# A step table for the scan units of a two-block image kernel, with the first half's finish at step 31

## The chip, the cores and the metric

The kernel runs on one core of a Trainium2 chip. The metric is device time in microseconds (us), lower is better. Five engines work side by side, each through its own instruction stream in order: PE (TensorE, matmuls), DVE (VectorE), ACT (ScalarE), POOL (GpSimd) and SP (SyncE, which here only issues DMAs). They meet only at semaphores: an instruction that waits holds up all that stands behind it on its engine.

## The reference

Input `x` is 16 images of 192 channels x 32 x 32 pixels, so 1024 positions each. Two blocks follow one another, each with a group norm before it and a residual around it:

```python
x = x + _L0_conv_ref(_gn(x), ...)   # projection, 3x3 depthwise conv + silu, chunked SSD scan (8 chunks of 128), layer norm, gate, projection
x = x + _L1_conv_ref(_gn(x), ...)   # projection, softplus, selective scan over 1024 positions, projection
```

The selective scan of the second block keeps 192 x 16 states:

```python
h = exp(d_t[..., None] * A) * h + (d_t * x_t)[..., None] * b_t[:, None, :]
y_t = einsum('bdn,bn->bd', h, c_t)
```

## The kernel before

**Two images at once.** `run(b, ...)` on each engine does a pass: the second block of image b beside the first block of image b + 1. There are 18 passes: b = -1 (first block of image 0 only), b = 0 to 14 with both, b = 15 (scan of the last image only) and b = 16 (its end). A pass is a loop `for s in range(SLOTS)` over 48 steps on every engine; the order within a step is the order of the code. No engine waits for a step as such, only for the semaphores of what it needs.

**The scan of image b** is cut into 48 units of 128 rows (32 channels x 4 states) by 512 positions, 24 for each half of the positions. Before the change a unit belongs to the step of its own number. A unit i passes through four engines: ACT makes its decay (L958, an Exp) in step i; DVE makes its input `wr` (L1236) in step i and scans it into `hst` (L1249) in step i + 1; POOL multiplies by C into `hc` (L768) in step i + 2; and PE adds two finished units to the output with four matmuls `bank<-hc,sel` (`sum_states`, called in every even step for the units i - 4 and i - 3). Rings tie them: a decay home is free when the unit before in it has been scanned, `hst` has three buffers, so the scan of unit i also waits for `hc` of unit i - 3 and, in the first half, for the `carry` copy of unit i - 3. That copy (L999, one column, the state that the second half starts from) is made by ACT for unit i - 2 at the end of step i, behind everything else of the step. Decays of the units below 8, 31 to 35 and from 38 on lie in PSUM banks, the others in three SBUF buffers (`dec`).

**The first block of image b + 1** sets what else a step does. Steps 0 to 2: group norm scale `xna`, `xnb` (L1063) and nine projections ("fills"). Steps 3, 5, 7 and 10 (`CONV_AT`): the four convs on PE, 24 or 48 calls of wcv matmuls each; conv u from the third on waits until conv u - 2 has left its banks. One step later (4, 6, 8, 11) ACT takes each out of PSUM with four Silus (`copy_conv`, L817 and L820), behind a table load, and loads the Exp/Ln table again (L823). Steps 3 to 8 also make dt: DVE softplus in step 5, PE's cumulative sum `csum` (`bank<-da,upper`) in step 6, `lndt` and its copies on DVE in step 6, Ln and two Exps on ACT in step 6, `ncs` on DVE in step 8. Steps 13 to 36: the eight SSD chunks, two steps each. Steps 37 to 40: statistics and group norm for the second block (means on PE in step 37, variances in 38, `xna` in 40). Steps 40 to 46: eight projections (`bank<-xna,wt1a` and `bank<-xnb,wt1b`). Steps 42 to 45 (`EARLY_AT`): statistics of the next input image.

**Finishing image b** (`finish`) adds the residual and the output projection: matmuls `x1a,ident`; `y1a,wo1a` and `y1b,wo1b`; `x1b,ident`; `y1a,wo1a` and `y1b,wo1b` again, in four steps from `END_AT`: 37 for the first half, 10 of the next pass for the second.

Names used below: stage A is steps 0 to 12, up to the first row transposes of the SSD (L1382); stage B is the SSD up to the last statistics (`mv`); stage C is the rest of the pass.

## Time and profile before

| what | value |
|---|---|
| median of 3 runs | 3541.34 us (3494.55 to 3560.41) |
| profiled execution, its own time | 3522.22 us |
| its span | 3520.5 us, mean granted TensorE clock 0.921 |
| PE busy | 3085.5 us, 88% |
| DVE busy | 2682.1 us, 76% |
| ACT busy | 1843.2 us, 52% |
| POOL busy | 1774.9 us, 50% |
| DMA queues | 27.4% of 16 engines' span |

The engine times are sums over the whole span, in which the passes repeat. No engine is full over all of it; which one sets the pace is read stage by stage. Matmuls overlap one another in the pipeline, so the PE figure is not a share of its peak.

### The profile page before, as it was taken

What the parts mean: (1) busy time and instruction counts of PE and PEld (TensorE: products, weight loads), DVE (VectorE), ACT (ScalarE), POOL (GpSimd) and SP (SyncE); (2) the same over time, 40 slices, a digit from 0 to 9 for tenths busy, and PEclk for the clock granted to TensorE, in tenths of its full rate; (3) what the DMA queues carried; (4) which work ended last, traced back from release to release, by engine and by line L of the source; (5) the groups of instructions that cost most, each with busy time, mean ns of one, the idle gap of its engine ahead of it and who ended that gap; (6) DMA issues with size and microseconds to landing.
All of it is one profiled execution on the core that took longest, in us unless ns stands there. A gap on an engine that the chain in (4) does not pass through costs nothing. (4 is left out here: it accounts for less than half of the span.)

```text
span 3520.5 us, 59688 instructions
## 1 busy us (share of the span) xinstructions
PE 3085.5 (88%) x19488; PEld 1739.0 (49%) x19488; DVE 2682.1 (76%) x3980; ACT 1843.2 (52%) x4315; POOL 1774.9 (50%) x1347
## 2 busy tenths in 40 slices
PE   4988889998898998889898898988889998898965
PEld 2655446364453735447364453735446364453710
DVE  1448878788787867868789787878868788787887
ACT  1536464653646546464564646546464563746542
POOL 2216545464554535545364554646545464555655
PEclk9999999998999989989899989989999998999976
DMA  3032141423214142141423314142141423215131
GB/s 63 11 108 75 46 129 50 116 70 97 85 46 144 40 136 65 58 116 39 134 70 96 85 46 127 58 129 76 59 117 46 121 70 108 73 45 147 37 103 66
DMA packets 103726, 290.86 MB, mean 83 GB/s; under 512 B 24941, under 2 KB 26588, under 8 KB 103388
## 3 DMA queue, kind: packets, MB, share of 16 engines
q1 hardware_dynamic: 103388, 286.71, 27.4%
q8 instruction: 169, 2.77, 0.3%
q14 instruction: 169, 1.38, 0.1%
HBM read 181.84 MB, written 39.85 MB: 63 GB/s over the span
## 5 line engine op out<-in xcount | busy, mean ns | idle before, releaser
L768 POOL TENSOR_TENSOR hc<-hst,bcrep 128x512 f32<-128x512 f32 x768 | 1204.4, 1568 | 1165.7 <-DVE hst L1249 1118.7
L854 ACT ACTIVATE ssd<-bank,ncs 128x128 f32<-128x128 f32 x1536 | 439.4, 385 | 230.1 <-PE bank L1298 229.3
L1298 PE MATMUL bank<-hc,sel 128*32 128x512 f32 x1536 | 447.7, 668 | 99.8 <-POOL hc L768 99.1
L1236 DVE TENSOR_TENSOR wr<-durep,bcrep 128x512 f32<-128x512 f32 x768 | 530.3, 691 | 3.1 <-DMA bcrep<-bc_rows 3.1
L1249 DVE TENSOR_TENSOR_SCAN hst<-dec,wr 128x512 f32<-128x512 f32 x256 | 389.7, 1522 | 93.6 <-ACT carry L999 60.3
L1298 PE MATMUL bank<-ssd 128*128 128x32 f32 (+1 forms) x3296 | 459.8, 293 | 0.0
L1298 PEld LDWEIGHTS bank<-ssd 128*128 128x128 f32 x3296 | 409.1, 197 | 17.6 <-issue 12.8
L958 ACT ACTIVATE bank<-durep,aneg 128x512 f32<-128x512 f32 x368 | 254.0, 690 | 300.4 <-DVE hst L1249 284.6
L1298 PE MATMUL bank<-ssd,wcv 64*32 64x512 f32 x5376 | 349.4, 599 | 0.0
L1298 PE MATMUL bank<-xna,wt0a 128*128 128x128 f32 (+3 forms) x1088 | 299.3, 377 | 36.4 <-DVE xnb L1064 35.4
L1249 DVE TENSOR_TENSOR_SCAN hst<-bank,carry,wr 128x512 f32<-128x512 f32 x240 | 306.1, 1275 | 11.9 <-ACT bank L958 2.5
L958 ACT ACTIVATE dec<-durep,aneg 128x512 f32<-128x512 f32 x400 | 292.7, 737 | 6.6 <-DVE hst L1249 4.1
L709 POOL TENSOR_TENSOR ssd<-ssd,wend 128x384 f32<-128x384 f32 x112 | 182.0, 1625 | 223.3 <-ACT ssd L901 223.3
L887 ACT ACTIVATE ssd<-bank,nbc,nwc 128x128 f32<-128x128 f32 x384 | 147.8, 454 | 274.8 <-PE bank L1442 274.8
L1298 PE MATMUL bank<-xnb,wt0b 128*128 128x128 f32 (+3 forms) x1088 | 287.2, 367 | 0.0
L1382 PE MATMUL bank<-ident,csum 128*128 128x128 f32 x1536 | 241.3, 281 | 21.4 <-ACT ssd L854 16.3
L1115 DVE TENSOR_TENSOR ssd<-ssd,bank 128x1536 f32<-128x1536 f32 x128 | 223.5, 1746 | 29.9 <-PE bank L1298 24.4
L1382 PEld LDWEIGHTS bank<-ident,csum 128*128 128x128 f32 x1536 | 187.1, 141 | 116.0 <-issue 50.4
L1298 PE MATMUL bank<-ssd,wo 128*128 128x128 f32 (+1 forms) x1536 | 215.7, 283 | 32.2 <-DVE x1b L1128 32.2
L1298 PEld LDWEIGHTS bank<-xna,wt0a 128*128 128x128 f32 (+1 forms) x1088 | 175.8, 195 | 135.3 <-issue 86.1
L1098 DVE TENSOR_TENSOR ssd<-ssd,bank 128x384 f32<-128x384 f32 x128 | 70.9, 554 | 208.1 <-PE bank L1298 208.1
L1298 PEld LDWEIGHTS bank<-ssd,wo 128*128 128x128 f32 (+1 forms) x1536 | 180.2, 167 | 64.6 <-DVE x1b L1128 37.6
(186 smaller groups left out, 4937.8 us busy)
## 6 DMA issues: line engine op xcount, KB each, us to landing
durep<-scratch SPq DMA_DIRECT2D x192, 512.0 KB, 3.9
bcrep<-bc_rows SPq DMA_DIRECT2D x128, 512.0 KB, 5.1
ssd<-stage SPq DMA_DIRECT2D x384, 140.4 KB, 2.9
ssd<-bcst SPq DMA_DIRECT2D x128, 74.4 KB, 2.7
xa<-in_x_dram SPq DMA_DIRECT2D x16, 512.0 KB, 4.2
scratch<-u SPq DMA_DIRECT2D x32, 256.0 KB, 2.5
scratch<-delta SPq DMA_DIRECT2D x32, 256.0 KB, 2.8
out_dram<-x1a SPq DMA_DIRECT2D x16, 512.0 KB, 4.6
```

The costliest lines, as they stand in the source:

```text
L709: nc.gpsimd.tensor_tensor(xw[:, c % 2, :].rearrange("p (h d) -> p h d", d=HD), xtok[:, c % 2, 0:DI].rearrange("p (h d) -> p h d", d=HD), b ...
L768: nc.gpsimd.tensor_tensor(hc[:, i % CRING, :], hst[:, i % HRING, :], bcrep[:, g, 1, :], ALU.mult).then_inc(hc_ready.sem, 1)
L854: ins = nc.scalar.activation(att[:, c % 2, h, :], bank[ROW_BANKS[r]][:, k * Q:(k + 1) * Q], ACT.Exp, bias=ncs[:, c, h:h + 1])
L887: ins = nc.scalar.activation(yzt[:, c % 2, m, :], bank[B_CBT][:, (m + 1) * Q:(m + 2) * Q], ACT.Identity, bias=nbc[:, m:m + 1], scale=nwc[: ...
L958: nc.scalar.activation(decay_of(i), durep[:, j % SLOTS_DU, 0, :], ACT.Exp, scale=aneg1[:, g * NB + k:g * NB + k + 1]).then_inc(decay_ready ...
L1098: nc.vector.tensor_tensor(y0[:, c % 2, :], yint[:, c % 2, :], bank[B_XY][:, 0:DI], ALU.add).then_inc(y0_ready.sem, 1)
L1115: nc.vector.tensor_tensor(a, a, bc(bank[B_CBT][:, 0:Q].unsqueeze(1), [P, NH, Q]), ALU.mult).then_inc(att_ready.sem, 1)
L1236: nc.vector.tensor_tensor(wr[:, i % WRING, :], durep[:, j % SLOTS_DU, 1, :], bcrep[:, g, 0, :], ALU.mult).then_inc(w_made.sem, 1)
L1249: nc.vector.tensor_tensor_scan(hst[:, i % HRING, :], decay_of(i), wr[:, i % WRING, :], carry[:, g:g + 1] if hf else 0.0, ALU.mult, ALU.add ...
L1298: return nc.tensor.matmul(out, lhsT, rhs, start=start, stop=stop, skip_group_check=True)
L1382: nc.tensor.matmul(ps[:, k * Q:(k + 1) * Q], bc(csum[:, 0, c, h:h + 1], [P, P]), ident[:, :], start=(k == 0), stop=False, is_transpose=Tru ...
```

## The change

A table says which units belong to a step. 28 steps from 12 on have one unit each; the first 12 have 17, and the last 8 have three. Steps 4, 6, 8 and 11 have 3, 2, 2 and 2 units. All loops over units go through `UNITS_AT`; the order of work for a given unit is kept, but of a step with several units an engine does the first stretch of its per-unit work for all of them. On ACT that means all decays of the step, then the first block's work of that step, then all carry copies. Besides that: the finish of the first half begins in step 31 and stands behind the first block's work of its step; the small Exp and Ln for dt come before `copy_conv` in step 4; PE's cumulative sum moves from step 6 (after a sum of units) to step 5; the statistics of the next image move one step earlier; decays of units 8 and 9 go to PSUM and those of 31 to 35 and 38 to 41 to `dec`; and copying `y1a` waits for the last finish.

```diff
-SLOTS = UNITS
+STEPS = 48
+UNITS_IN_STEP = [1, 1, 1, 1, 3, 1, 2, 1, 2, 1, 1, 2] + 28 * [1] + [0, 1, 0, 1, 0, 0, 1, 0]
+UNITS_AT = [range(sum(UNITS_IN_STEP[:s]), sum(UNITS_IN_STEP[:s + 1])) for s in range(STEPS)]
...
-EARLY_AT = 42
+EARLY_AT = 41
...
-END_AT = (37, 10)
+END_AT = (31, 10)
...
+FRONT_UNITS, LAST_UNITS = 10, 42
...
-    if i < 8 or i >= 38:
+    if i < FRONT_UNITS or i >= LAST_UNITS:
         return i % 2
-    return 6 + i % 2 if 31 <= i < 36 else None
+    return None
...
-                for u, at in enumerate(CONV_AT):
-                    if s == at + 1:
-                        copy_conv(n, u)
                 if s == 4:
...
                     nc.scalar.activation(dtl[:, :, :], dte[:, :, :], ACT.Ln, bias=1.0).then_inc(dtl_ready.sem, 1)
+                for u, at in enumerate(CONV_AT):
+                    if s == at + 1:
+                        copy_conv(n, u)
...
-            def copy_wide(n, hf):
+            def copy_wide(n, hf, prev):
+                if hf or prev:
+                    act.wait_ge(o1_ps.sem, o1_ps.at(n, 2 * hf))
...
-                        decay(b, s, end, first)
+                        for i in UNITS_AT[s]:
+                            decay(b, i, end, first)
...
-                        if 2 <= s < HU + 2:
-                            act.wait_ge(scanned.sem, scanned.at(b, s - 1))
+                        for i in UNITS_AT[s]:
+                            if 2 <= i < HU + 2:
+                                act.wait_ge(scanned.sem, scanned.at(b, i - 1))
...
-                if s == 6:
+                if s == 5:
                     pe.wait_ge(da_ready.sem, da_ready.at(n, 1))
...
-                        if s == END_AT[0]:
-                            pe.wait_ge(scanned.sem, scanned.at(b, 36))
-                        finish(b, s, 0, par)
                     if first:
                         first_block(b + 1, s, end if scan else None)
+                    if scan:
+                        finish(b, s, 0, par)
```

The order on PE between the second and the third conv of a pass with both blocks (steps 5 to 7). The wcv rows are convs, `hc,sel` are sums of two units, `da` is the cumulative sum for dt. Before:

```order
L1298 MATMUL bank<-ssd,wcv 32x512 x24
L1298 MATMUL bank<-hc,sel 32x512 [waits hc_ready]
L1298 MATMUL bank<-hc,sel 32x512
L1298 MATMUL bank<-da,upper 128x96 [waits fill_copied,da_ready]
L1298 MATMUL bank<-da,ones 128x96
L1298 MATMUL bank<-ident 128x1 [waits im_landed1,conv_done]
L1298 MATMUL bank<-ssd,wcv 32x512 x48
```

And of the change:

```order
L1310 MATMUL bank<-ssd,wcv 32x512 x24
L1310 MATMUL bank<-da,upper 128x96 [waits fill_copied,da_ready]
L1310 MATMUL bank<-da,ones 128x96
L1310 MATMUL bank<-hc,sel 32x512 [waits hc_ready]
L1310 MATMUL bank<-hc,sel 32x512
L1310 MATMUL bank<-hc,sel 32x512 [waits hc_ready]
L1310 MATMUL bank<-hc,sel 32x512
L1310 MATMUL bank<-ident 128x1 [waits im_landed1,conv_done]
L1310 MATMUL bank<-ssd,wcv 32x512 x48
```

The cumulative sum now comes first, and two sums instead of one stand ahead of the third conv: before it was that of units 2 and 3, now those of units 4 and 5 and of units 6 and 7.

The order on ACT in steps 5 and 6, around the Silus of the second conv. `bank<-durep,aneg` are decays into PSUM, `carry<-hst` the carry copies. Before:

```order
L958 ACTIVATE bank<-durep,aneg 128x512 [waits scanned]
L999 COPY carry<-hst 128x1 [waits scanned]
L958 ACTIVATE bank<-durep,aneg 128x512 [waits scanned]
L820 ACT_TABLE_LOAD
L820 ACTIVATE bs<-bank,cb 32x512 [waits conv_ps]
...
L823 ACT_TABLE_LOAD
L874 ACTIVATE dtl<-dtl 128x96 [waits csum_ready]
L875 ACTIVATE cexp<-csum 128x192
L876 ACTIVATE wend<-wend 128x96
L999 COPY carry<-hst 128x1 [waits scanned]
```

And of the change:

```order
L964 ACTIVATE bank<-durep,aneg 128x512 [waits scanned]
L1009 COPY carry<-hst 128x1 [waits scanned]
L964 ACTIVATE bank<-durep,aneg 128x512 [waits scanned]
L964 ACTIVATE bank<-durep,aneg 128x512 [waits scanned]
L828 ACT_TABLE_LOAD
L828 ACTIVATE bs<-bank,cb 32x512 [waits conv_ps]
...
L831 ACT_TABLE_LOAD
L882 ACTIVATE dtl<-dtl 128x96 [waits csum_ready]
L883 ACTIVATE cexp<-csum 128x192
L884 ACTIVATE wend<-wend 128x96
L1009 COPY carry<-hst 128x1 [waits scanned] x2
```

Ahead of the Silus there are now the decays of units 8 and 9 where there was that of unit 6, and behind them the carries of units 6 and 7 where there was that of unit 4. The decay of unit 9 goes to the bank that unit 7's decay has, so it waits for the scan of unit 7.

The order on PE at the end of the statistics for the second block, from step 37 on. `mv` and `gq` are the means and variances. Before:

```order
L1298 MATMUL bank<-x1a,ident 128x512 [waits scanned]
...
L1298 MATMUL bank<-hc,sel 32x512 [waits hc_ready]
L1298 MATMUL bank<-hc,sel 32x512
L1298 MATMUL bank<-y1a,wo1a 128x512 [waits y1_copied,x1_ps]
L1298 MATMUL bank<-y1b,wo1b 128x512
...
L1298 MATMUL bank<-gq,ga 128x1 [waits gdev_ready]
...
L1298 MATMUL bank<-y1a,wo1a 64x512 [waits y1_copied,x1_ps]
L1298 MATMUL bank<-y1b,wo1b 64x512
L1298 MATMUL bank<-xna,wt1a 128x512 [waits xn_ready]
```

And of the change:

```order
L1310 MATMUL bank<-mv,ga 128x1 [waits stats_ready]
...
L1310 MATMUL bank<-xcm,diag1b 64x512 [waits p1_copied,y1_copied]
...
L1310 MATMUL bank<-gq,ga 128x1 [waits gdev_ready]
...
L1310 MATMUL bank<-hc,sel 32x512 [waits hc_ready]
L1310 MATMUL bank<-hc,sel 32x512
L1310 MATMUL bank<-xna,wt1a 128x512 [waits xn_ready]
```

The six groups of the finish are gone from this place; they stand in steps 31 to 34, between the gates and output projections of the last two chunks.

## Rows read from the trace of the kernel before

**Rows 1.** One line of code, L1063: count, ns least/median/most, first and last start.

```profile
L1063 DVE TENSOR_SCALAR xna<-xa,gm,gr x16: 811/1051/1909, 56.7 to 3179.2; 128x1024 f32<-128x1024 f32 x16
```

**Rows 2.** Stretches: us, busy PE, PEld, DVE, ACT, POOL (x), PEclk, DMA share, GB/s.

```profile
1281.90:1342.30 60.40, 55.51 (x459) 20.80 (x459) 39.85 (x48) 41.96 (x74) 24.13 (x16) 0.94 0.46 123
1342.30:1456.60 114.30, 102.39 (x659) 76.28 (x658) 93.61 (x152) 58.01 (x170) 68.27 (x54) 0.94 0.17 54
1456.60:1494.10 37.50, 33.73 (x100) 11.54 (x100) 32.90 (x50) 14.44 (x24) 17.88 (x13) 0.86 0.32 105
...
812.90:858.50 45.60, 41.77 (x100) 14.90 (x100) 32.77 (x49) 14.51 (x25) 16.90 (x12) 0.70 0.30 97
```

**Rows 3.** Timeline of PE, stage A: start us, us, operation [idle before <-releaser].

```profile
1310.88 5.36 PE L1298 MATMUL bank<-ssd,wcv 64*32 64x512 f32 x48
1316.16 1.05 PE L1298 MATMUL bank<-hc,sel 128*32 128x512 f32 x4
...
1317.91 5.38 PE L1298 MATMUL bank<-ssd,wcv 64*32 64x512 f32 x96
...
1326.98 1.05 PE L1298 MATMUL bank<-hc,sel 128*32 128x512 f32 x4 [2.71 <-POOL hc L768]
...
1329.71 6.43 PE L1298 MATMUL bank<-ssd,wcv 64*32 64x512 f32 x96
...
1342.29 0.65 PE L1382 MATMUL bank<-ident,csum 128*128 128x128 f32 x4
```

**Rows 4.** Timeline of DVE, stage A.

```profile
1316.87 1.28 DVE L1148 TENSOR_SCALAR dtl<-dt 128x96 f32<-128x96 f32 x1
...
1318.86 1.22 DVE L1249 TENSOR_TENSOR_SCAN hst<-bank,wr 128x512 f32<-128x512 f32 x1
...
1322.81 1.08 DVE L1155 TENSOR_TENSOR ncs<-dtl,csum 128x96 f32<-128x96 f32 x1 [0.17 <-ACT dtl L874]
...
1330.96 1.23 DVE L1249 TENSOR_TENSOR_SCAN hst<-dec,wr 128x512 f32<-128x512 f32 x1 [2.37 <-ACT carry L999]
```

**Rows 5.** Timeline of ACT, stage A.

```profile
1316.41 0.69 ACT L958 ACTIVATE bank<-durep,aneg 128x512 f32<-128x512 f32 x1 [1.91 <-DVE hst L1249]
1317.12 1.28 ACT L820 ACT_TABLE_LOAD   x1
1318.41 0.68 ACT L820 ACTIVATE bs<-bank,cb 32x512 f32<-32x512 f32 x1
...
1322.94 0.27 ACT L876 ACTIVATE wend<-wend 128x96 f32<-128x96 f32 x1
1323.11 0.18 ACT L999 COPY carry<-hst 128x1 f32<-128x1 f32 x1
```

**Rows 6.** Timeline of POOL, stage A.

```profile
1320.16 1.64 POOL L768 TENSOR_TENSOR hc<-hst,bcrep 128x512 f32<-128x512 f32 x1 [2.08 <-DVE hst L1249]
```

**Rows 7.** Timeline of PE and of DVE, end of stage B.

```profile
1451.23 1.73 PE L1298 MATMUL bank<-ssd,wo 128*128 128x128 f32 x12 [1.70 <-DVE x1b L1128]
...
1454.82 0.28 DVE L1127 TENSOR_TENSOR x1a<-bank,xa 128x128 f32<-128x128 f32 x1
```

**Rows 8.** Timeline of PE, stage C.

```profile
1459.61 2.08 PE L1298 MATMUL bank<-y1a,wo1a 128*128 128x512 f32 x2
...
1462.67 0.38 PE L1298 MATMUL bank<-gq,ga 128*128 128x1 f32 x2
...
1469.23 1.12 PE L1298 MATMUL bank<-xna,wt1a 128*128 128x512 f32 x2
...
1487.74 0.38 PE L1298 MATMUL bank<-gq,ga 128*128 128x1 f32 x2 [2.21 <-DVE gq L1055]
```

**Rows 9.** Timeline of DVE, stage C.

```profile
1456.64 0.20 DVE L1047 BATCH_NORM_AGGREGATE mv<-st 128x2 f32<-128x12 f32 x1
...
1460.14 0.16 DVE L1055 TENSOR_TENSOR gq<-gd,mv 128x2 f32<-128x2 f32 x1
...
1465.80 1.76 DVE L1063 TENSOR_SCALAR xna<-x1a,gm,gr 128x1024 f32<-128x1024 f32 x1
```

More of the change, by code:

```diff
@@ L771, in run @@
             def run(b, par, scan, end, first, more):
-                for s in range(SLOTS if scan or first else 2):
-                    if s < 2:
-                        if end:
-                            states_by_c(b - 1, UNITS - 2 + s, False)
-                    elif scan:
-                        states_by_c(b, s - 2, end)
+                for s in range(STEPS if scan or first else 2):
+                    for i in UNITS_AT[s]:
+                        if i < 2:
+                            if end:
+                                states_by_c(b - 1, UNITS - 2 + i, False)
+                        elif scan:
+                            states_by_c(b, i - 2, end)
                     if scan:
@@ L987, in run @@
                 mid_step = Steps(act, act_mid_steps, b)
-                for s in range(SLOTS if scan or first else END_AT[1] + END_STEPS):
+                for s in range(STEPS if scan or first else END_AT[1] + END_STEPS):
                     if scan:
-                        decay(b, s, end, first)
+                        for i in UNITS_AT[s]:
+                            decay(b, i, end, first)
                     if scan:
@@ L1577, in finish, with sums @@
                     mm(o, wo1b[r, c], y1b[r, :], False, True).then_inc(o1_ps.sem, 1)
-            def run(b, par, scan, end, first, more):
-                for s in range(SLOTS if scan or first else END_AT[1] + END_STEPS):
-                    if s in (0, BATCH):
-                        if end:
-                            sum_states(b - 1, BATCHES - 2 + s // BATCH, False)
-                    elif scan and s > 2 and (s - 2) % BATCH == 0:
-                        sum_states(b, (s - 2) // BATCH - 1, end)
-                    for hf in range(2):
-                        if scan and s == hf * HU + WIDE + 3:
-                            start_rest(b, hf)
+            def sums(b, i, scan, end):
+                if i in (0, BATCH):
+                    if end:
+                        sum_states(b - 1, BATCHES - 2 + i // BATCH, False)
+                elif scan and i > 2 and (i - 2) % BATCH == 0:
+                    sum_states(b, (i - 2) // BATCH - 1, end)
+                for hf in range(2):
+                    if scan and i == hf * HU + WIDE + 3:
+                        start_rest(b, hf)
+            def run(b, par, scan, end, first, more):
+                for s in range(STEPS if scan or first else END_AT[1] + END_STEPS):
+                    for i in UNITS_AT[s]:
+                        sums(b, i, scan, end)
                     if end:
                         if scan and s == END_AT[1]:
-                            pe.wait_ge(scanned.sem, scanned.at(b, 8))
+                            pe.wait_ge(scanned.sem, scanned.at(b, FRONT_UNITS))
                         if not scan and s == END_AT[1]:
```

40 lines of the change are left out of this document (21 added, 19 removed).

## Prediction, made before the changed kernel ran

> **What bounds the kernel now.** The busy shares come first. No engine is full, so the next view is the passes: sixteen starts of `xna` from `xa`, one for each pass from b = -1 to 14 [rows 1]. From the first start, 56.7, to the last, 3179.2, it is 208 us a pass, the short first one (no scan) among them. I cut one pass with both blocks (b = 5, 212.2 us) into its stages [rows 2]. Stage A takes 60.4 us and PE is busy for 55.5 of them; there PE sets the pace. Stage B, the SSD, takes 114.3 us, PE 102.4 and DVE 93.6: the two hand chunks to each other. Stage C takes 37.5 us, and DVE is busy for 32.9, PE for 33.7. The granted clock matters in C: in the pass from 644.6 on the same stage took 45.6 us at 0.70 against 37.5 at 0.86 [rows 2]. Whatever is gained or lost below happens in 15 passes (b = 0 to 14).
>
> The timeline of stage A shows how it is driven. PE does a conv in 5.4 us and then a sum of two units in 1.05, back to back, with one hole: 2.71 us before the sum at 1326.98, where `hc` was late [rows 3]. `hc` is late because DVE and ACT hold one another up. ACT's Silus of a conv take a table load of 1.28, four times 0.68 and a second load; only behind them come the small Exps and the carry copy [rows 5], and DVE stands idle for such a carry, 2.37 us at 1330.96 [rows 4]. So a scan three units ahead of a carry can't run during the Silus. That is what the added units run into.
>
> **Stage A, step by step, in times of this pass.** Up to the end of the first conv (1308.6) nothing changes. Then PE has one more sum than before ahead of the second conv, so this ends at 1317.2 and not at 1316.24 [rows 3], and the cumulative sum, which took about 0.65 between 1317.2 and the next conv's start [rows 3], ends at 1317.85.
>
> DVE: the scan of unit 5 needs the carry of unit 2, behind the first Silus, which is there at about 1313.1. The scan (1.22), `wr` (0.67), five small operations of dt (an estimate of 1.4), the scan of unit 6 and its `wr` take DVE to 1318.3. Then `lndt`, which took 1.28 and ended with POOL's `hc`; here POOL starts the `hc` of unit 6 at about 1317.7 and holds it until 1319.3. From the end of `lndt` to the next scan it took 0.71, in which the cumulative sum is copied and subtracted [rows 4]. So unit 7 is scanned from 1320.1 to 1321.3, and its `hc` (1.64, [rows 6]) ends at 1323.0. PE has done the sum of units 4 and 5 by 1318.9 and must wait for that `hc` in order to do the sum of 6 and 7 ahead of the third conv: **4.1 us idle**. After the sum the third conv starts at 1324.3, not at 1317.91 [rows 3].
>
> ACT: the decay of unit 9 waits for the scan of unit 7 (1321.3) and takes 0.7; then come load, Silus, load (1.28 + 2.8 + 1.28), the three small ones (0.75) and the carry of unit 6 (0.18) [rows 5]. That makes 1328.5. DVE scans unit 9 then (to 1329.8) and POOL's `hc` ends at 1331.5. PE is through with the third conv at 1329.7, or about 1330.8 if it runs as slowly after its hole as the fourth did after the hole of 2.71 (6.43 against 5.38, [rows 3]); I take 1330.8, so **0.7 idle** before the sum of 8 and 9, which ends at 1332.6. On DVE `ncs` waits for POOL (1.08 where its neighbours take 0.25, [rows 4]), until 1331.8; then two scans with a `wr` between them, 1.9 to 2.8 each, put the `hc` of unit 11 at 1337.5: **4.9 idle** before the sum of 10 and 11. The fourth conv follows the first matmul of the finish, and ends at 1346.8 where it was 1336.14 [rows 3]. One sum more than before (two in place of one) follows until the first row transposes. They start at 1354.1, not at 1342.29 [rows 3]. Stage A loses **11.8 us**: three more sums, 3.15, and 7.0 more idle (9.7 less the old 2.71), 1.1 for the slow conv, and half a microsecond of rounding. From below: without the wait of `lndt` for POOL, without a slow conv and with the quickest scans it is 8. From above, with ACT and DVE half a microsecond later in each link, 14.
>
> One price is disputed, that of a table load. Here the Silu starts 0.01 after its load of 1.28 ends [rows 5]. By the Trainium skill, "ScalarE: Activation LUTs", What ACT_TABLE_LOAD costs, a switch of sets is the load and a drain of 1.38 us as well, some 2.66 together. By that rule the two switches on the chain would add 2.8 us a pass and 41 us in all; no gap of that size stands behind this load, so the sum goes by the row.
>
> **Stage B.** The number of units in a step stays as it was. The first half's finish, 6.4 us of PE at full clock, now stands in steps 31 to 34. PE had holes there, 1.70 before the last output projection for instance [rows 7]. Laid among them, the six groups make that projection end 3.5 later; the residual that waited for it started 1.86 after its old end of 1452.96 [rows 7], so 1.7 remains. I take **+1.8**, between 0 (the holes hold it all) and 3.
>
> **Stage C.** The finish no longer stands before the variances: `gq` was ready at 1460.30 [rows 9] and PE came to it at 1462.67, behind `y1a,wo1a` [rows 8]. 2.3 of that go at once. Then the `xna` of 1465.80 [rows 9] and the projections that could start only at 1469.23, behind another two groups of the finish [rows 8], come sooner: I get 3.7 us from the last statistics to the first projection, and more in passes where the clock is low there, as in the C of 45.6 us [rows 2]. From the first projection to the end it was 24.9 [rows 2, 8], with eight projections of 2.05, four sums, a start of the second accumulation and the two statistics of the next image. The new order has two sums less inside it and no such start, and DVE has 5 units (1.95 each) less to do, which makes 22 to 22.5: PE still waits for `gq` of the next image, about 2.7 where it was 2.21 [rows 8], since softplus, `u1` and one scan come first on DVE. Stage C gains 3.7 and 2.5, **6.2 us**. From below 3.5, if only the finish's way is saved; from above 9.6, if all PE waits go.
>
> **Sum.** 11.8 + 1.8 - 6.2 = +7.4 us a pass, by 15 passes 111 us. 3522 + 111 = 3633 us. That stands against the profiled execution's 3522.22; the median of the runs is 19 us above it, which would make 3652. I say 3635.
>
> **Rivals.**
>
> *PE never waits in A.* If ACT and DVE ran so far ahead that the sums of step 7, 8 and 10 found their `hc`, A would lose only the three sums and win the old 2.71. With B and C as above that is 3.15 - 2.71 + 1.8 - 6.2 = -4.0 a pass, 3463 us; with C at its best of 9.6 it is -7.4, 3412 us, over 3% faster. It decides at one point: the decay of unit 9 would have to be made without the cumulative sum's copy on DVE ahead of it. Against it: that copy stands before the scan of unit 7 in DVE's order, and the decay is queued before the Silus on ACT. 0.05.
>
> *Half of it.* The holes come out shorter, A loses 4 to 8, C gains 6 to 9: between -5 and +3 a pass, so 3450 to 3570, no change that can be told. For it: DVE is busy for only 39.9 of A's 60.4 us [rows 2], so some of what I lay on it may fit in earlier. 0.20.
>
> *The clock falls.* The new holes, 4.1 and 4.9, are longer than the 2.71 after which a conv took 6.43. If the third and fourth conv ran at 1.2 and not 2.4 GHz throughout, each would take 10.8: 4.3 and 5.4 more than my sum has, 9.7 a pass, 3780 us. The Trainium skill, "TensorE: Matmul & The Clock Gate", What's actually happening, has the array fall to half rate after idling, as that row does. For it the rows of stage C at 0.70; against it the sums and the conv between the holes. 0.09.
>
> *My sum.* 0.66.
>
> **The numbers.** About 2% is what a measurement of this kernel can tell. Range: from 3545, which leaves out the first rival and most of the second, to 3725, where A is at 14, C at 3.5 and B at 3 (+13.5 a pass). That keeps about eight cases in ten. Slower by over 2% is my sum but for its lowest part, and the clock: 0.72. Within 2%: 0.23. Faster: 0.05.
>
> **What would show it.** In stage A: PE idle for 3 to 5 us before the sum ahead of the third conv and again before the one ahead of the fourth, with POOL's `hc` as releaser; the Silus of the second conv about 5 us later after their conv than now; first row transposes at 70 to 74 us from the pass's start instead of 60.4. In stage B nothing but a longer end. In stage C `gq,ga` within 0.2 us of `gq`, and 30 to 33 us in all. I would be wrong if the sums of units 6, 7 and 10, 11 start without a wait, or if the stretch from the first row transposes to the last statistics shrinks, which nothing in these rows provides for.

## The result: 3.5% slower, and the profile after

| what | before | after |
|---|---|---|
| median | 3535.4 us (4 runs, 3494.6 to 3560.4) | 3655.7 us (4 runs, 3651.3 to 3661.7) |
| ratio | | 1.0352, 95% interval 1.0310 to 1.0394 |
| span of the profiled execution, granted clock | 3520.5, 0.921 | 3649.5, 0.895 |
| PE busy | 3085.5 | 3107.1, 85% |
| DVE busy | 2682.1 | 2750.8, 75% |
| ACT, POOL busy | 1843.2, 1774.9 | 1847.8, 1753.3 |

The change costs 129 us in the profiled execution. No engine got much more to do; what grew is the time in which they wait for one another. In the tables of this document a stage is the mean over the 14 passes b = 0 to 13, from the start of `xna` to the next start, taken from the starts in the traces. C1 is the stretch from the last statistics to the first projection, C2 the rest of C. "Low" is how many us of a pass PE was granted half the clock, worked out from the granted clock of four stretches in each pass (length x (1 - clock) x 2). "Masking" is DVE's multiplication `ssd<-ssd,bank` of 128x1536, one for each chunk of the SSD.

| kernel | A | B | C1 | C2 | pass | low |
|---|---|---|---|---|---|---|
| before | 60.1 | 109.6 | 14.5 | 26.3 | 210.4 | 28 |
| after | 73.5 | 114.1 | 10.2 | 20.8 | 218.6 | 40 |

So A lost 13.5, B lost 4.6, C gained 9.8: 8.2 a pass, 115 in 14 passes. The first pass, b = -1, got shorter (177.1 to 166.5), and what follows the sixteenth `xna` got 25.5 longer (341.2 to 366.8). Together 129.

The pass b = 10 of after, in four stretches: A; the start of B up to the masking of the third chunk; the rest of B; C. Columns: stretch, its us, PE busy (instructions), granted clock, DMA share, GB/s. It answers to [rows 2].

```profile
2405.70:2480.00 74.30, 62.75 (x471) 0.86 0.54 142
2480.00:2513.20 33.20, 27.24 (x144) 0.85 0.25 87
2513.20:2593.20 80.00, 77.22 (x526) 1.00 0.10 28
2593.20:2624.20 31.00, 26.50 (x78) 0.78 0.23 72
```

PE's timeline in stage A of this pass, which answers to [rows 3]. Columns: start, us, operation, idle before it and its releaser.

```profile
2435.83 5.36 PE L1310 MATMUL bank<-ssd,wcv 64*32 64x512 f32 x48
2442.36 0.46 PE L1310 MATMUL bank<-da,upper 128*128 128x96 f32 x2 [1.17 <-DVE da L1155]
...
2442.97 1.05 PE L1310 MATMUL bank<-hc,sel 128*32 128x512 f32 x4
2448.93 1.92 PE L1310 MATMUL bank<-hc,sel 128*32 128x512 f32 x4 [4.91 <-POOL hc L775]
...
2451.30 6.92 PE L1310 MATMUL bank<-ssd,wcv 64*32 64x512 f32 x96
2458.16 1.05 PE L1310 MATMUL bank<-hc,sel 128*32 128x512 f32 x4
2463.04 1.92 PE L1310 MATMUL bank<-hc,sel 128*32 128x512 f32 x4 [3.83 <-POOL hc L775]
2464.89 2.08 PE L1310 MATMUL bank<-x1a,ident 128*128 128x512 f32 x2
...
2467.11 5.85 PE L1310 MATMUL bank<-ssd,wcv 64*32 64x512 f32 x96
```

The two foretold holes are there: 4.91 ahead of the third conv and 3.83 ahead of the fourth, both for POOL's `hc`. The matmuls behind each run slowly: sums of 1.92 where they take 1.05, a conv of 6.92 where it takes 5.38. What makes `hc` late stands on ACT and DVE, [rows 4, 5] of before. First ACT, around the Silus of the second conv:

```profile
2439.95 0.17 ACT L1009 COPY carry<-hst 128x1 f32<-128x1 f32 x1
2443.51 0.69 ACT L964 ACTIVATE bank<-durep,aneg 128x512 f32<-128x512 f32 x1 [3.39 <-DVE hst L1259]
2447.21 0.69 ACT L964 ACTIVATE bank<-durep,aneg 128x512 f32<-128x512 f32 x1 [3.01 <-DVE hst L1259]
2447.92 1.28 ACT L828 ACT_TABLE_LOAD   x1
2449.22 0.68 ACT L828 ACTIVATE bs<-bank,cb 32x512 f32<-32x512 f32 x1
...
2453.92 0.27 ACT L1009 COPY carry<-hst 128x1 f32<-128x1 f32 x2
```

And DVE in the same stretch:

```profile
2438.06 1.22 DVE L1259 TENSOR_TENSOR_SCAN hst<-bank,wr 128x512 f32<-128x512 f32 x1 [6.72 <-ACT carry L1009]
...
2439.78 1.27 DVE L1079 TENSOR_SCALAR dtu<-dte 128x96 f32<-128x96 f32 x1
...
2443.97 1.27 DVE L1158 TENSOR_SCALAR dtl<-dt 128x96 f32<-128x96 f32 x1
...
2454.12 1.22 DVE L1259 TENSOR_TENSOR_SCAN hst<-bank,wr 128x512 f32<-128x512 f32 x1 [4.47 <-ACT carry L1009]
...
2459.17 2.11 DVE L1259 TENSOR_TENSOR_SCAN hst<-dec,wr 128x512 f32<-128x512 f32 x1
...
2477.41 1.23 DVE L1259 TENSOR_TENSOR_SCAN hst<-dec,wr 128x512 f32<-128x512 f32 x1 [4.37 <-ACT carry L1009]
```

ACT waits 3.39 and 3.01 for scans before it may make the next decays, and its Silus are queued behind those decays: they end at 2452.0, although their conv ended at 2441.2. DVE in turn waits 6.72, 4.47 and 4.37 for carry copies that stand behind the Silus. On the mean of 14 passes such waits make 15.3 us of stage A on DVE, where they made 4.3 before. In the page of the whole execution the scans with a decay in PSUM and no carry input have 208.4 us of idle before them, 167.6 of it for a carry:

```profile
L1259 DVE TENSOR_TENSOR_SCAN hst<-bank,wr 128x512 f32<-128x512 f32 x160 | 195.5, 1222 | 208.4 <-ACT carry L1009 167.6
L1310 PE MATMUL bank<-hc,sel 128*32 128x512 f32 x1536 | 458.3, 700 | 195.9 <-POOL hc L775 195.9
```

PE's timeline at the border of B and C, for [rows 8]:

```profile
2593.50 0.38 PE L1310 MATMUL bank<-mv,ga 128*128 128x1 f32 x2 [2.02 <-DVE mv L1058]
...
2594.48 1.97 PE L1310 MATMUL bank<-xcm,diag1b 128*64 128x512 f32 x2
2596.89 0.59 PE L1310 MATMUL bank<-gq,ga 128*128 128x1 f32 x2 [0.44 <-DVE gq L1065]
...
2603.36 2.08 PE L1310 MATMUL bank<-xna,wt1a 128*128 128x512 f32 x2 [2.76 <-DVE xnb L1074]
```

No finish stands in the way any more: the variances run as soon as `gq` is there.

### The profile page after: what moved, and what is told of

Read it like the earlier page. It is cut to its first block and busy times, and to the rows that moved or that the text cites. A ratio compares the mean times of both kernels' runs of the same rounds, so it can differ in the third digit from the quotient of the medians.

```text
span 3649.5 us, 59703 instructions
## 1 busy us (share of the span) xinstructions
PE 3107.1 (85%) x19488; PEld 1756.8 (48%) x19488; DVE 2750.8 (75%) x3980; ACT 1847.8 (51%) x4315; POOL 1753.3 (48%) x1347
## 3 DMA queue, kind: packets, MB, share of 16 engines
q14 instruction: 169, 1.38, 0.1%
## 5 line engine op out<-in xcount | busy, mean ns | idle before, releaser
L1310 PE MATMUL bank<-ssd 128*128 128x32 f32 (+1 forms) x3296 | 481.1, 301 | 2.1 <-DVE ssd L1125 1.9
L1310 PEld LDWEIGHTS bank<-ssd 128*128 128x128 f32 x3296 | 433.5, 207 | 11.4 <-issue 5.5
L1259 DVE TENSOR_TENSOR_SCAN hst<-dec,carry,wr 128x512 f32<-128x512 f32 x288 | 408.0, 1417 | 20.6 <-ACT dec L964 10.0
L964 ACT ACTIVATE dec<-durep,aneg 128x512 f32<-128x512 f32 x512 | 368.3, 731 | 69.0 <-DMA durep<-scratch 49.8
L1310 PE MATMUL bank<-ssd,wcv 64*32 64x512 f32 x5376 | 368.1, 630 | 0.0
L1259 DVE TENSOR_TENSOR_SCAN hst<-bank,wr 128x512 f32<-128x512 f32 x160 | 195.5, 1222 | 208.4 <-ACT carry L1009 167.6
L964 ACT ACTIVATE bank<-durep,aneg 128x512 f32<-128x512 f32 x256 | 175.9, 691 | 278.9 <-DVE hst L1259 249.7
L716 POOL TENSOR_TENSOR ssd<-ssd,wend 128x384 f32<-128x384 f32 x112 | 141.8, 1266 | 285.4 <-ACT ssd L909 285.4
L1394 PE MATMUL bank<-ident,csum 128*128 128x128 f32 x1536 | 256.0, 293 | 13.7 <-ACT ssd L862 10.7
L1310 PEld LDWEIGHTS bank<-xna,wt0a 128*128 128x128 f32 (+1 forms) x1088 | 173.6, 194 | 173.1 <-issue 110.5
L1310 PEld LDWEIGHTS bank<-hc,sel 128*32 128x32 f32 x1536 | 56.6, 114 | 391.6 <-POOL hc L775 275.2
```

What stands on the lines that cost most here:

```text
L716: nc.gpsimd.tensor_tensor(xw[:, c % 2, :].rearrange("p (h d) -> p h d", d=HD), xtok[:, c % 2, 0:DI].rearrange("p (h d) -> p h d", d=HD), b ...
L964: nc.scalar.activation(decay_of(i), durep[:, j % SLOTS_DU, 0, :], ACT.Exp, scale=aneg1[:, g * NB + k:g * NB + k + 1]).then_inc(decay_ready ...
L1259: nc.vector.tensor_tensor_scan(hst[:, i % HRING, :], decay_of(i), wr[:, i % WRING, :], carry[:, g:g + 1] if hf else 0.0, ALU.mult, ALU.add ...
L1310: return nc.tensor.matmul(out, lhsT, rhs, start=start, stop=stop, skip_group_check=True)
L1394: nc.tensor.matmul(ps[:, k * Q:(k + 1) * Q], bc(csum[:, 0, c, h:h + 1], [P, P]), ident[:, :], start=(k == 0), stop=False, is_transpose=Tru ...
```

## The experiments

Each was timed beside the kernel before on the same chip; the ratio is to that. All stage values follow in one table.

| run | median us | ratio (95%) | A | B | C1 | C2 | pass | low | last part |
|---|---|---|---|---|---|---|---|---|---|
| before | 3535.4 | 1 | 60.1 | 109.6 | 14.5 | 26.3 | 210.4 | 28 | 341.2 |
| after | 3655.7 | 1.035 (1.031 to 1.039) | 73.5 | 114.1 | 10.2 | 20.8 | 218.6 | 40 | 366.8 |
| e1, old table | 3460.5 | 0.976 (0.971 to 0.981) | 58.2 | 112.6 | 10.2 | 25.3 | 206.3 | 27 | 354.6 |
| e2, carry first | 3499.2 | 0.988 (0.983 to 0.993) | 67.5 | 110.3 | 10.2 | 20.6 | 208.6 | 28 | 356.0 |
| e3, copies behind | 3647.2 | 1.030 (1.026 to 1.035) | 72.6 | 114.7 | 10.2 | 21.0 | 218.5 | 41 | 370.8 |
| e4, Silu first | 3560.4 | 1.006 (1.000 to 1.012) | 72.4 | 111.1 | 10.2 | 20.6 | 214.2 | 35 | 365.3 |
| e5, e1 + carry first | 3485.9 | 0.987 (0.980 to 0.994) | 58.8 | 114.0 | 10.3 | 25.3 | 208.4 | 32 | 351.4 |
| e6, three moves | 3552.4 | 1.007 (1.003 to 1.010) | 69.7 | 110.5 | 10.2 | 20.9 | 211.3 | 36 | 361.8 |
| e7, e1, finish at 37 | 3593.0 | 1.017 (1.011 to 1.024) | 61.0 | 115.9 | 12.3 | 26.3 | 215.5 | 42 | 355.3 |
| e8, three units | 3492.2 | 0.990 (0.984 to 0.996) | 64.3 | 109.9 | 10.8 | 22.7 | 207.8 | 34 | 353.4 |
| e9, e7, decays in PSUM | 3532.9 | 0.998 (0.996 to 1.001) | 60.7 | 112.9 | 11.8 | 26.5 | 211.8 | 34 | 344.9 |
| e10, busy holes in A | 3635.7 | 1.029 (1.023 to 1.035) | 72.3 | 114.2 | 10.2 | 20.8 | 217.5 | 30 | 360.1 |
| e11, e1, busy in C | 3471.6 | 0.980 (0.974 to 0.986) | 58.5 | 114.4 | 12.1 | 22.9 | 207.9 | 22 | 351.4 |
| e12, e2 + Silu first | 3503.7 | 0.989 (0.985 to 0.993) | 67.0 | 110.4 | 10.2 | 20.6 | 208.1 | 28 | 352.1 |

### The table alone

```diff
-UNITS_IN_STEP = [1, 1, 1, 1, 3, 1, 2, 1, 2, 1, 1, 2] + 28 * [1] + [0, 1, 0, 1, 0, 0, 1, 0]
+UNITS_IN_STEP = 48 * [1]
-FRONT_UNITS, LAST_UNITS = 10, 42
+FRONT_UNITS, LAST_UNITS = 8, 38
```

> The change with one unit in every step (48 times 1) and decays in PSUM for units below 8 and from 38 on; the finish stays in steps 31 to 34, the statistics of the next image a step early. Theory (the loss of stage A is the units laid on steps 4, 6, 8 and 11): stage A is back at 60 us a pass from 73.5; from the last statistics to the first projection 10 to 11 us stay from 14.5, since that gain is the finish's; the rest of stage C goes back towards 26 (24 to 26), since that gain is the units'. B 110 to 112. Sum 206 to 209 a pass, 3440 to 3500 us in all. Rival (the tail's gain is the finish's alone): the rest of C stays at 21 and the whole comes to under 3420. Rival (the moved finish costs as much in B as it saves): 3520.

With the table go back the homes of the decays of units 8, 9 and 38 to 41. Measured: 3460.5. The rest of the change is a gain of 2.4%, the lowest median of all versions; the table takes 195 us away from it. A falls from 73.5 to 58.2, C2 rises by 4.6 only: the table pays 15.4 us in A, and 1.5 in B, for 4.6 in C.

### Three moves inside the new table

The carry copies come out from behind the Silus:

```diff
                         for i in UNITS_AT[s]:
                             decay(b, i, end, first)
+                            if 2 <= i < HU + 2:
+                                act.wait_ge(scanned.sem, scanned.at(b, i - 1))
+                                nc.scalar.copy(carry[:, i - 2:i - 1], hst[:, (i - 2) % HRING, HALF - 1:HALF]).then_inc(carried.sem, 1)
```

> The change, but ACT makes each carry copy right behind the decay of its unit's slot, ahead of the first block's work of the step (so ahead of the Silus). Theory: the scans of units 5, 9 and 16 no longer wait for a carry behind the Silus (6.7, 4.5 and 4.4 us idle on DVE); PE's hole before the sum ahead of the third conv shrinks from 4.9 to 2.6, since that one hangs on the cumulative sum; the one ahead of the fourth stays at about 4, since units 10 and 11 stand behind ncs. Stage A 67 to 69 from 73.5, 3565 us (3540 to 3590). Rival (the carries are not what holds DVE, its decays are): no change, 3650.

Measured 3499.2. DVE's waits for a carry in stage A fall from 15.3 to 2.7 us a pass, PE's hole ahead of the third conv from 4.9 to 2.8 on the mean (2.6 expected). A is 67.5, inside what was expected, and the time is 66 us below the expectation because B gave back its loss too (114.1 to 110.3) and the last part 10.8. One move of a copy of 0.2 us takes 156 us off the changed kernel.

On DVE the cumulative sum's copies of step 6 move behind the scans:

```diff
-                if s == 6:
-                    step(nc.vector.tensor_scalar(lndt[:, :, :], dt0[:, :, :], TINY, None, ALU.max))
...
+                    if first and s == 6:
+                        cumulative(b + 1, step)
```

> The change, but on DVE in step 6 lndt, the copy of the cumulative sum and wend stand behind the scans of units 7 and 8. Theory: unit 7 is scanned 2 us earlier, PE's hole ahead of the third conv is 2.9 instead of 4.9, all behind it comes 2 us earlier: stage A 71.5, 3620 us. Rival (that hole is the Silus' doing, not the cumulative sum's): hole and time unchanged, 3650.

Measured 3647.2: a miss, nothing to speak of. The hole ahead of the third conv did shrink as expected, to 3.2, and that conv starts 8.2 after the second's end where it was 10.1, but the fourth starts 9.1 after the third's end where it was 8.8, and B is as long as in the changed kernel. My point of decision for the rival in which PE never waits, the copy ahead of the scan of unit 7, wasn't what decides.

On ACT the Silus of the second conv move ahead of the decays of step 6:

```diff
+                    if first and s == CONV_AT[1] + 1:
+                        copy_conv(b + 1, 1)
                     if scan:
                         for i in UNITS_AT[s]:
                             decay(b, i, end, first)
```

> The change, but on ACT in step 6 the Silus of the second conv stand ahead of the decays of units 8 and 9. Theory: the hole ahead of the third conv stays (4.9), the Silus come 6 us sooner after their conv, unit 9 is scanned 4 us sooner, and the hole of 3.8 ahead of the fourth conv goes. Stage A 69 to 70, 3590 us. Rival (both holes are one delay by DVE): both stay, 3650.

Measured 3560.4, better than expected, but not where it was expected. PE's timeline in stage A of this kernel:

```profile
2421.14 1.92 PE L1312 MATMUL bank<-hc,sel 128*32 128x512 f32 x4 [4.92 <-POOL hc L775]
...
2429.84 2.17 PE L1312 MATMUL bank<-hc,sel 128*32 128x512 f32 x8
...
2433.12 5.38 PE L1312 MATMUL bank<-ssd,wcv 64*32 64x512 f32 x96
2440.15 1.05 PE L1312 MATMUL bank<-hc,sel 128*32 128x512 f32 x4 [1.65 <-POOL hc L775]
...
2445.72 1.57 PE L1312 MATMUL bank<-hc,sel 128*32 128x512 f32 x4 [1.41 <-POOL hc L775]
```

The first hole stays at 4.92, the second is gone, and new ones of 1.65 and 1.41 open behind the fourth conv, 3.3 us a pass on the mean: A keeps 72.4. The gain lies in B, 3.0 us, of which 2.7 in its start, where the granted clock is 0.891 in place of 0.845. So the two holes have two causes, the first the carries and the second the late Silus, and removing one moves the wait.

All three together:

```diff
+                            if 2 <= i < HU + 2:
...
+                        copy_conv(b + 1, 1)
...
+                        cumulative(b + 1, step)
```

> The table of the change with the three moves together: carries behind the decays, Silus of the second conv ahead of the decays of step 6, the cumulative sum's copies behind the scans of step 6. Each alone gave 3499.2, 3560.4 and 3647.2 against 3655.7 of the changed kernel. Theory (two holes with two causes: carries for the first, late Silus for the second): they add up for the most part, A from 73.5 to 63 to 66, B near 110, C at 30.7, a pass of some 205, 3450 to 3480. Rival (one chain through DVE and ACT, which each move only shortens at one end): nothing is gained over the best one, 3500, A stays at 67.5.

Measured 3552.4, outside both ranges. The first hole is gone, but ACT's timeline shows what the three together do:

```profile
2381.37 0.18 ACT L1005 COPY carry<-hst 128x1 f32<-128x1 f32 x1
2384.48 0.28 ACT L882 ACTIVATE dtl<-dtl 128x96 f32<-128x96 f32 x1 [2.93 <-DVE wend L1148]
...
2385.10 0.71 ACT L964 ACTIVATE dec<-durep,aneg 128x512 f32<-128x512 f32 x1
```

The Ln for dt waits 2.93 for `wend`, which DVE now makes behind its scans, and the decays of step 7 and 8 are queued behind it; the fourth conv starts 14.2 after the third's end. One run more tells whether it is that:

```diff
+                            if 2 <= i < HU + 2:
...
+                        copy_conv(b + 1, 1)
```

> The changed kernel with two of the three moves: carries behind the decays, and the Silus of the second conv ahead of the decays of step 6; the cumulative sum's copies stay ahead of the scans. With all three moves the time was 3552.4, worse than the 3499.2 of the carries alone: the third conv then began 2.0 us after the second's end, without a hole, but the fourth 14.2 after the third's end (7.1 with carries alone). Theory (the copies put behind the scans make the Ln and Exps of dt late on ACT, and with them everything queued behind them, the carries too): without that move the fourth conv starts 5 to 8 us after the third's end, A at 65 to 68, 3470 to 3500. Rival (the Silus ahead of the decays do the harm as soon as the carries are early): the gap of 14 stays, A near 70, 3540 to 3560.

Measured 3503.7, A 67.0, the fourth conv 6.5 after the third: the copies behind the scans did the harm, and the Silus ahead of the decays add nothing once the carries are early.

### The old table again, and a milder one

```diff
-UNITS_IN_STEP = [1, 1, 1, 1, 3, 1, 2, 1, 2, 1, 1, 2] + 28 * [1] + [0, 1, 0, 1, 0, 0, 1, 0]
+UNITS_IN_STEP = 48 * [1]
...
+                            if 2 <= i < HU + 2:
```

> The table of one unit a step again, the finish at step 31, and on ACT each carry copy right behind the decays of its step. In the run with the old table alone (3460.5) the fourth conv still started 4.4 us after the third had ended, where a sum takes 1.05. Theory (the carry copies behind the Silus hold DVE's scans back, whatever the table): stage A falls from 58.2 to 55.5 to 57, B by 1 to 2, so about 3 us less in each of 15 passes: 3415 to 3435. Rival (only a step with several units makes a carry late; with one unit a step the wait lies under PE's work): A stays within 0.5 us, and the time at 3460.

Measured 3485.9, ratio 0.987 against 0.976 of the old table alone: the rival held for A (58.8 against 58.2), and the time is no better. With one unit a step a late carry lies under PE's work. The 25 us on top are not in a wait of that kind: B's start took 32.0 in place of 30.5, at a clock of 0.864 in place of 0.929.

```diff
+UNITS_IN_STEP = [1, 1, 1, 1, 2, 1, 1, 1, 1, 1, 1, 2, 2] + 27 * [1] + [0, 1, 1, 1, 0, 0, 1, 1]
+FRONT_UNITS, LAST_UNITS = 8, 42
```

> A milder table, three units moved in place of five, into steps 4, 11 and 12 ([1,1,1,1,2,1,1,1,1,1,1,2,2], 27 ones, [0,1,1,1,0,0,1,1]), so that no second unit stands in the Silu steps 6 and 8; carries behind the decays as in the run beside it with the old table. Theory (a unit taken out of C is worth 0.9 us there and costs half a sum, 0.5, in A, as long as it doesn't stand in steps 6 and 8): A 1.5 to 3 us longer than with the old table and carries first, C 2 to 3 shorter, the time within 20 us of it. Rival (any unit moved into the front makes the holes again): A longer by 5 or more, 3460 or above, 30 us or more over the old table with carries first.

Measured 3492.2, within 20 us of the old table with early carries, as the theory said, but by larger terms than it had: A is 5.5 longer (64.3), which is the rival's term, B 4.1 shorter and C 2.0 shorter. PE waits before the fourth conv are gone (it starts 2.0 after the third's end), and 4.3 us of waiting for `hc` stand behind it. So the units are no cheaper outside steps 6 and 8; the wait only comes later.

### What the finish does, and what the decays do

```diff
-END_AT = (31, 10)
+END_AT = (37, 10)
```

(with the old table)

> The table of one unit a step and the finish of the first half back at step 37, so that of the change only the small moves are left (cumulative sum in step 5, dt ahead of the Silus, statistics one step earlier, decays of units 31 to 35 in SBUF, finish behind the first block's work). Theory (the finish's place is what shortens the way from the last statistics to the first projection, 14.5 to 10.2, and costs B something): that stretch returns to 13.5 to 14.5, B falls from 112.6 to 110 to 111, the pass from 206.3 to 207.5 to 209, the time 3480 to 3505. Rival (the gain is the small moves'): 3460, as with the finish at step 31.

Measured 3593.0, far above both. C grows by 3.1, as C1 goes from 10.2 to 12.3 and C2 by 1.0. C1 keeps the other half of its gain over the 14.5 of before, with the finish behind the block's work: the means and variances go ahead of it, and its last two matmul pairs now run behind the first projections. But B gets longer too, 115.9, and A, 61.0, with the same work. Both go with the clock: PE is at half clock for 42 us a pass here and for 27 with the finish at 31. On the mean the first conv starts 25.1 after the pass's start, at a granted clock of 0.78 up to there, and not 22.3, at 0.88; the start of B takes 33.7 in place of 30.5.

The end of B was not helped. From the last chunk's masking to the last statistics it took 22.7 in before, 25.4 after, and 25.3 here, with the finish away. Hence the next one, which adds to this one only:

```diff
-    return None
+    return 6 + i % 2 if 31 <= i < 36 else None
...
+                if first and i == 31:
+                    act.wait_ge(row_exp.sem, row_exp.at(n + 1, NRB * NCH))
...
+                        if s == END_AT[0]:
+                            pe.wait_ge(scanned.sem, scanned.at(b, 36))
```

> As the run with the old table and the finish back at step 37 (3593.0), but the decays of units 31 to 35 lie in PSUM again, as before the change. In every variant so far, with the finish at 31 or at 37, it took 25.1 to 25.5 us from the start of the last chunk's masking on DVE to the last statistics, where before it took 22.7; so the finish, on which my sum laid 1.8 us of stage B, can't be it. Theory (the scans of units 31 to 35 with both inputs in SBUF are slower beside POOL, and hold DVE up where it sets the pace): that stretch returns to 22.5 to 23.3 and the time falls by 2 to 3 us a pass, to 3545 to 3565. Rival (it is something else that all variants share, such as the finish behind the first block's work): the stretch stays at 25 and the time at 3593.

The two added waits belong to the place: the banks are used by the first block's work and by the finish. Measured 3532.9, 60 us less and below the expected range, and the stretch is back at 22.7. DVE's scans in it, one pass with the decays in SBUF (columns: group, count, busy us, mean ns, idle before):

```profile
L1259 DVE TENSOR_TENSOR_SCAN hst<-dec,carry,wr 128x512 f32<-128x512 f32 x7 | 11.6, 1651 | 0.2
```

and one with them in PSUM:

```profile
L1261 DVE TENSOR_TENSOR_SCAN hst<-bank,carry,wr 128x512 f32<-128x512 f32 x5 | 6.3, 1270 | 0.1
L1261 DVE TENSOR_TENSOR_SCAN hst<-dec,carry,wr 128x512 f32<-128x512 f32 x2 | 2.6, 1280 | 0.1
```

11.6 us of scans against 8.9: the 2.7 us by which B's end was longer. A pass is 3.7 shorter; the 1.0 beyond that lies in C1, A and the start of B. The last part of the execution, in which only scans are left, falls from 355.3 to 344.9 with it.

### Is it the clock?

Matmuls that compute nothing fill the holes of the changed kernel:

```diff
+                        if first and scan and i == 10:
+                            pe.wait_ge(conv_done.sem, conv_done.at(b + 1, 2))
+                            keep_busy(CONV_BANKS[2][0], 4)
+                        if first and scan and i == 14:
+                            pe.wait_ge(conv_done.sem, conv_done.at(b + 1, 4))
+                            keep_busy(CONV_BANKS[3][0], 3)
                         sums(b, i, scan, end)
```

> The changed kernel, its order untouched, with matmuls that compute nothing laid into PE's two holes: four of about 0.87 us ahead of the sum of units 6 and 7 (hole of 4.9) and three ahead of the sum of 10 and 11 (hole of 3.8). In the changed kernel the granted clock of stage A is 0.894 (before 0.940), that from the first row transposes to the third chunk's masking 0.845 (before 0.946), and that stretch takes 33.5 us where it takes 28.8 in passes of before at 1.00. Theory (PE's idle time in the holes is what brings the clock down, in A and behind it): third and fourth conv 5.4 in place of 6.6 and 5.8, the stretch behind at 28 to 30, a pass 4 to 7 us shorter, 3550 to 3595. Rival (the clock at the start of B falls for the idle time there, before the state matmuls): stage A shortens by 1 us, the stretch stays at 33, 3640. A third way (more work brings it down further): 3655 or above.

PE's timeline, the fillers being `wcv,ident`:

```profile
2438.32 1.05 PE L1310 MATMUL bank<-hc,sel 128*32 128x512 f32 x4
2439.30 3.70 PE L1310 MATMUL bank<-wcv,ident 128*128 128x512 f32 x8
2444.28 1.05 PE L1310 MATMUL bank<-hc,sel 128*32 128x512 f32 x4 [1.28 <-POOL hc L775]
2445.26 0.38 PE L1310 MATMUL bank<-ident 128*128 128x1 f32 x2
2445.57 5.38 PE L1310 MATMUL bank<-ssd,wcv 64*32 64x512 f32 x96
2452.45 1.05 PE L1310 MATMUL bank<-hc,sel 128*32 128x512 f32 x4 [1.49 <-POOL hc L775]
2453.43 2.84 PE L1310 MATMUL bank<-wcv,ident 128*128 128x512 f32 x6
2458.37 1.29 PE L1310 MATMUL bank<-hc,sel 128*32 128x512 f32 x4 [2.09 <-POOL hc L775]
```

Measured 3635.7: the rival's value. The third conv runs at 5.38 now and A's clock is 0.956 in place of 0.894, but A shortens by 1.2 only, since `hc` comes no sooner, and the start of B stays at 33.5 with a clock of 0.856. So the idle time in A's holes does bring the clock down in A, that is worth about 1 us a pass, and filling it does nothing for B. PE's wait for the first state matmul of B, the idle time that the rival names, was not filled and stays at 3.33 to 4.62.

The same in stage C of the fastest version:

```diff
                 if s == PRE_AT + 1:
+                    if again is not None:
+                        keep_busy(5, 3)
                     group_means(n, 1)
...
                         if k == 0:
+                            if again is not None:
+                                keep_busy(5, 2)
```

> The fastest variant so far (table of one unit a step, finish at 31; 3460.5) with matmuls that compute nothing in front of two waits of stage C: three ahead of the means of the last statistics (idle 3.1 us) and two ahead of the first projection (1.35). There C runs at a granted clock of 0.78 and its first projections take 2.05 where others take 1.1. Theory (idle time brings the clock down): C at 0.88 or above, its projections at 1.1 to 1.3, C 1.5 to 4 us shorter than 35.5, and a stage A behind it that begins at the full clock: 3400 to 3440. Rival (the clock there follows something else, or the added matmuls only stand in the way): C stays within 1 us of 35.5 and the time at 3450 to 3480.

Measured 3471.6. C's clock rose from 0.778 to 0.893 as expected; C shortened by 0.5 us only, the rival's line. C2 fell by 2.4 and C1 rose by 1.8: the fillers stood in the way of the variances and sums. And B's start was slow in 9 of 14 passes, 32.3 on the mean against 30.5. Matmuls that compute nothing do raise PE's clock, but this kernel gains little by it where DVE or ACT set the pace.

## Why the prediction was right, and where its terms were off

**The whole.** 3635 was forecast, 3655.7 measured, inside the range; slower, as the likeliest case. Against the profiled execution's own time of 3651.3 the sum gave 3633. The terms behind it are less good than the total: 11.8 + 1.8 - 6.2 forecast, 13.5 + 4.6 - 9.8 measured, +8.2 for +7.4. Misses of 1.7, 2.8 and 3.6 us a pass cancel, so that the total came this close is in good part luck; that A's loss outweighs C's gain is not.

**Stage A, 11.8 forecast, 13.5 measured.** The mechanism held: e1 takes it away with the table (15.4 us), e2 takes 6.1 away with the place of the carries alone. The added idle time was nearly right in sum: 10.5 us before the cumulative sum and the sums of units on the mean of 14 passes, 2.7 in before, so 7.8 more for the 7.0 forecast. Its parts were less so: 4.1, 0.7 and 4.9 forecast, 4.9, 0 and 4.2 on the mean (4.91 and 3.83 in the pass shown), and 1.2 before the cumulative sum that I didn't have. There `dtu` took 1.27 on DVE, beside POOL's `hc`, where I had laid all five dt operations at 1.4; they took 2.4. The rest of the difference is clock: two sums at 1.92 in place of 1.05, and a third conv of 6.6 in place of 5.4 on the mean; I had slowed one conv by 1.1 and no sum. The Silus of the second conv end 10.1 after it on the mean (10.8 in the pass shown), where they ended 4.2 after it: 5.9 later, about 5 forecast. The row transposes start 74.3 after the pass's start, 73.5 on the mean (70 to 74 forecast).

**Stage B, 1.8 forecast, 4.6 measured, by another cause.** This is the step that failed. I laid the finish's groups among PE's holes at the end of B; e7, with the finish back at step 37, has 25.3 us there, e1 with the finish at 31 has 25.5, and all variants with those decays in SBUF have 25.1 to 25.5. e9 shows what it is: the decays of units 31 to 35 in SBUF, 2.7 us. I named that move in the change and priced it at nothing. The other 1.9 is the start of B: up to the third chunk 33.5 for 30.2, at a clock of 0.845 for 0.946, of which the chunks between give 1.5 back. The late carries reach into it. DVE leaves stage A late (its wait of 4.37 at 2477.41 above), and PE waits for the first state matmul:

```profile
2490.95 0.91 PE L1310 MATMUL bank<-state,cs_ 128*128 128x384 f32 x2 [3.43 <-DVE state L1089]
```

That wait is 3.33 to 4.61 us in the 14 passes, 2.38 to 2.78 in before. In e2, with the carries early, it is 1.22 to 1.68 in 13 of 14 passes, and the start of B takes 30.1 at a clock of 0.922. In the changed kernel the clock falls in every pass, during this wait or within 1.5 us behind it. So my sum had no term for what A's delay does to B. Whether it is this wait that brings the clock down, no run shows by itself.

**Stage C, -6.2 forecast, -9.8 measured.** C1 gained 4.3 for the 3.7 forecast. In e7 and e9, where the finish stands at step 37 but behind the block's work, C1 is 2.2 and 2.7 shorter than in before and C2 no shorter; so about half of C1's gain goes with that order and the other small moves, and the rest with the finish's leaving C. The 5.5 of C2 had 2.5 in the sum: 4.6 are the table's (e1), where PE is busy for 19.8 us in place of 23.7. The term with the wrong sign is PE's wait for `gq` of the next image, which I raised from 2.21 to 2.7. It is 0.9 on the mean, and 2.2 in before: that alone is 1.8 of the 3.0 that I missed. I had put softplus, `u1` and a scan ahead of it on DVE. But it isn't the units taken out in front of it either, since with the old table (e1) the wait is 0.9 as well, here 1.01:

```profile
1440.14 0.38 PE L1310 MATMUL bank<-gq,ga 128*128 128x1 f32 x2 [1.01 <-DVE gq L1065]
```

What e1 and the changed kernel share and before lacks is, above all, the statistics one step earlier. That this is the cause is a reading; no run changed it alone.

**What the sum did not have.** The 15 passes were taken as equal. The first got 10.6 shorter, the last part 25.5 longer than before, though my term for it held only one pass of 7.4. About 10 of that are the decays in SBUF, by e7 and e9. 12 more go with the table (366.8 against 354.6). At the start of the last image's second pass DVE's timeline has this:

```profile
3496.89 1.28 DVE L1259 TENSOR_TENSOR_SCAN hst<-bank,carry,wr 128x512 f32<-128x512 f32 x1
3506.05 0.69 DVE L1246 TENSOR_TENSOR wr<-durep,bcrep 128x512 f32<-128x512 f32 x1 [7.88 <-DMA bcrep<-bc_rows]
```

I read it as part of those 12: e2 and e3, with the new table, have such a wait too (7.38 and 7.22), and e1, e7 and e9 have none. No run took it away alone.

**The rivals.** PE never waits: it waited, and e3 and e6 show that the copy which I made its turning point doesn't decide. Half of it: A lost more than 8. The clock falls: the two convs did not run at 1.2 GHz throughout, 6.6 and 5.8 against the 10.8 of that case. Yet the clock was a larger part than my 1.1 us: half clock for 40 us a pass, 28 before. The Trainium skill, "TensorE: Matmul & The Clock Gate", What's actually happening, has the array fall to half rate after idling; e10 agrees for the convs behind the holes (5.38 once filled), and [rows 3] did so before.

**The table load.** Behind the load of 1.28 at 2447.92 the first Silu starts at 2449.22, 0.02 after its end. A drain of 1.38 beside it, as the Trainium skill, "ScalarE: Activation LUTs", What ACT_TABLE_LOAD costs, has it, does not show here, neither behind the load nor ahead of it, where the decay ends 0.02 before it starts. Half of the 128 loads of this trace have the next instruction within 0.02 us of their end.

## What to carry to other kernels

When a schedule table moves more units of one chain into a step, look at what its engines queue behind other work in that step: a copy of 0.2 us behind Silus held DVE for 4 to 7 us, and moving the copy was worth 156 us. Read each buffer that changes its memory as a change of price, too: five decays that moved from PSUM to SBUF to make room for the better placed finish cost 60 us in the two runs that differ by them and the waits that go with their place. And test the parts of a bundle singly: the parts without the table were 2.4% faster than before, the whole was 3.5% slower.

## What the runs showed of the hardware

**A scan's time depends on where its decay lies.** With the decay in PSUM all 3904 scans of the 14 traces take 1.21 to 1.29 us, whether POOL is at work or not. With `dec` in SBUF it is 1.20 to 1.29 where POOL isn't at work when the scan starts (2596 scans), and up to 2.15, 1.67 on the mean, where it is (4252 scans). At 2459.17 above it is 2.11. POOL's `hc` ran from 2458.66 to 2460.20 there:

```profile
2458.66 1.54 POOL L775 TENSOR_TENSOR hc<-hst,bcrep 128x512 f32<-128x512 f32 x1 [1.58 <-DVE hst L1259]
```

The scan began 1.03 before that end and took 0.90 longer than the 1.21 of a scan beside an idle POOL. The Trainium skill, "SBUF — State Buffer", Who interferes with whom, says that a VectorE instruction with two SBUF inputs contends with a GpSimd instruction that reads SBUF, and that the later one is blocked until the other ends. These rows agree, for the scan too.

**The clock falls in one pass and not in another after the same idle time.** Two passes of before, PE at the start of B. In the first the state matmul comes after 2.48 us of idle, at full clock:

```profile
1134.96 1.05 PE L1298 MATMUL bank<-hc,sel 128*32 128x512 f32 x4
1138.48 0.91 PE L1298 MATMUL bank<-state,cs_ 128*128 128x384 f32 x2 [2.48 <-DVE state L1079]
```

and in the second after 2.47, at half:

```profile
1349.23 1.05 PE L1298 MATMUL bank<-hc,sel 128*32 128x512 f32 x4
1352.76 1.65 PE L1298 MATMUL bank<-state,cs_ 128*128 128x384 f32 x2 [2.47 <-DVE state L1079]
```

The same matmuls stand ahead of both. The stretch from the first row transposes to the third chunk's masking took 28.8 us in the first of these passes, at a clock of 1.00, and 34.7 in the second, at 0.80. Before has 10 of 14 passes of the quick kind. After has none (30.9 to 36.5), but there the wait is longer, 3.33 us and more. The old table with the finish at 37 has none either (30.1 to 34.9), though this wait, 2.46 in most passes, and the order of its matmuls there are those of before. So with equal idle time some 5 us of a pass hang on something that none of these edits aims at, and differences of 25 us between variants, as between e1 and e5, can't be put down to an edit by its own place alone. What decides between the two kinds is left open. In e10 PE's idle time before the cumulative sum and the sums of stage A was 6.3 us in place of 10.5, and the start of B as slow, so that part of it does not decide.
